# First expert weights in 32 tensors, and the expert numbers of the last tiles read once, two tiles ahead

## The reference

```
x = x + attention(layernorm(x))            # 4 heads, dk 128, dv 64, a scan over 512 tokens
h = layernorm(x)
probs = softmax(h @ router_w.T)            # 8 experts
vals, idx = top_k(probs, 2)
out = 0
for e in range(8):
    w = sum(where(idx == e, vals, 0), -1)
    out += w[:, None] * (gelu(h @ w1[e].T) @ w2[e].T)   # w1[e]: 1024 x 256, w2[e]: 256 x 1024
x = x + out
```

## Time and profile before

| | us |
|---|---|
| median of three executions | 939.12 |
| the profiled execution | 941.82 |
| its span, first to last instruction | 940.0 |
| PE busy | 860.5 (92%) |
| VectorE busy | 627.1 (67%) |
| ScalarE busy | 604.0 (64%) |
| GpSimd busy | 440.4 (47%) |
| mean granted TensorE clock | 0.972 |

### The profile page before, as it was taken

One profiled execution on the slowest core, in us unless ns is written; L12 is line 12 of the kernel. 1 busy time (PEld: TensorE's weight loads), 2 busy tenths in 40 slices (PEclk: granted clock), 3 DMA queues, 4 the chain that ended last, 5 costly groups with the idle time before them and its releaser, 6 DMA issues. The chain is left out here.

```text
span 940.0 us, 29903 instructions
## 1 busy us (share of the span) xinstructions
PE 860.5 (92%) x9998; PEld 677.0 (72%) x9999; DVE 627.1 (67%) x1832; ACT 604.0 (64%) x1645; POOL 440.4 (47%) x433
## 2 busy tenths in 40 slices
PE   3789999999999999999987899999999999998883
PEld 2468887788877888788866677777777777766661
DVE  4578898698988989888874845555554555543441
ACT  3478888788888888888776644555544555433430
POOL 2164555577677677677556532233322233312222
PEclk9899999899999999999987999999999999999997
DMA  6012322233233332332232342233322223312212
GB/s 207 2 58 80 87 64 76 74 98 96 89 103 89 96 104 82 102 103 76 70 108 91 127 69 47 46 49 57 50 47 45 45 45 59 52 29 47 35 18 29
DMA packets 50152, 66.96 MB, mean 71 GB/s; under 512 B 6448, under 2 KB 34352, under 8 KB 50032
## 3 DMA queue, kind: packets, MB, share of 16 engines
q1 hardware_dynamic: 36064, 46.20, 17.1%
q0 software_dynamic: 13424, 18.10, 11.2%
q10 hardware_dynamic: 544, 1.05, 0.3%
HBM read 41.84 MB, written 23.48 MB: 69 GB/s over the span
## 5 line engine op out<-in xcount | busy, mean ns | idle before, releaser
L764 ACT ACTIVATE inverse_levels<-ps 128x512 f16<-128x512 f32 (+1 forms) x324 | 169.7, 539 | 181.6 <-PE ps L1499 154.8
L746 POOL DMA_INDIRECT out<-inverse_levels,yidx x71 | 119.0, 1676 | 277.8 <-DVE inverse_levels L2180 194.8
L1126 PE MATMUL ps<-inverse_levels,w_hi 128*128 128x256 f16 (+1 forms) x1376 | 199.6, 255 | 1.5 <-issue 1.3
L1126 PE MATMUL ps<-inverse_levels,w_lo 128*128 128x256 f16 (+1 forms) x688 | 169.2, 254 | 0.0
L2153 DVE SCALAR_TENSOR_TENSOR KpAT<-kq_wvg,inverse_levels 128x512 f16<-128x512 f32 (+1 forms) x144 | 98.8, 688 | 95.2 <-ACT inverse_levels L764 95.1
L1126 PE MATMUL ps<-w_s,inverse_levels 128*128 x426 | 141.3, 381 | 14.9 <-ACT inverse_levels L764 9.0
L1126 PEld LDWEIGHTS ps<-inverse_levels,w_hi 128*128 x1376 | 119.7, 98 | 19.0 <-issue 2.4
L1126 PE MATMUL ps<-w_s,KpAT 128*128 x426 | 116.6, 274 | 0.0
L1026 ACT ACTIVATE kq_wvg<-ps 128x512 f32<-128x512 f32 (+1 forms) x144 | 85.0, 590 | 46.4 <-PE ps L1126 40.3
L2176 DVE TENSOR_SCALAR inverse_levels<-ps,gate 128x256 f32<-128x256 f32 x71 | 31.1, 480 | 102.8 <-PE ps L1126 102.8
L1734 DVE CAST_PREDICATED inverse_levels<-mask_s,ps 128x256 f16<-128x256 int8 x192 | 82.2, 428 | 18.0 <-PE ps L1126 12.7
(11 more groups left out here) (237 smaller groups left out, 1932.3 us busy)
## 6 DMA issues: line engine op xcount, KB each, us to landing
wst<-w SPq DMA_DIRECT2D x58, 256.0 KB
inverse_levels<-eye SPq DMA_DIRECT2D x35, 256.0 KB, 2.7
x_s<-x SPq DMA_DIRECT2D x32, 128.0 KB, 2.6
out<-x_s SPq DMA_DIRECT2D x32, 128.0 KB, 1.7
x_s<-routed_rows SPq DMA_DIRECT2D x7, 260.0 KB, 2.7
Lh<-routed_rows SPq DMA_DIRECT2D x7, 260.0 KB, 2.7
Vp<-routed_rows SPq DMA_DIRECT2D x7, 260.0 KB, 2.9
rowA<-routed_rows SPq DMA_DIRECT2D x7, 260.0 KB, 2.9
```

The costliest lines, as they stand in the source:

```text
L746: pool.indirect_dma_start(out=out, out_offset=bass.IndirectOffsetOnAxis(ap=yidx[:, q, a:a + 1], axis=0), in_=yrow[:, q % 2, a, :], in_offs ...
L764: return act.activation(dst, src, ACT.Copy, scale=scale)
L1126: return pe.matmul(dst, lhsT, rhs, start=start, stop=stop, **kw)
```

## The change

Three things change.

The two tensors w1_hi and w1_lo become 32, one for each part, k and m, of eight experts by 128 columns. The host lays out w1 in the new order, so that the pieces that are loaded are still 64 of 512 columns, and `split_hi` and `split_lo` write each to its place (`w1_place`).

In `up` the address of a weight is taken from the tensor of its part, k and m at e * 128.

For split tiles `parts_of` no longer reads the expert numbers. `load_experts(t + 2)` reads them in `down` of tile t, behind the fifth of the eight blocks m (m = 4), and keeps them for `up` and `down` of that tile.

```
-        w1_hi = sb("w1_hi", [P, KC * E * HID], fp16)
-        w1_lo = sb("w1_lo", [P, KC * E * HID], fp16)
+        w1_hi, w1_lo = [[[sb(f"w1_{part}_{k}_{m}", [P, E * P], fp16) for m in range(KH)] for k in range(KC)] for part in ("hi", "lo")]
...
+        def w1_place(at):
+            n = E * P // PIECE
+            return at // (KH * n), at // n % KH, slice(at % n * PIECE, (at % n + 1) * PIECE)
...
-                    cols = slice(at * PIECE, (at + 1) * PIECE)
-                    lo, hi, src = w1_lo[:, cols], w1_hi[:, cols], wst[:, :]
+                    k, m, cols = w1_place(at)
+                    lo, hi, src = w1_lo[k][m][:, cols], w1_hi[k][m][:, cols], wst[:, :]
...
+            loaded = {}
+            def load_experts(t):
+                if t < TILES and split(0, t):
+                    loaded[t] = [(expert_of(*divmod(t, 4), a), slice(a * P, (a + 1) * P)) for a in range(halves(*divmod(t, 4)))]
             def parts_of(i, q):
+                if split(i, q) and i * 4 + q in loaded:
+                    return loaded[i * 4 + q]
...
                         for k in range(KC):
-                            off = e * HID + (k * E * HID + m * P)
-                            wh, wl = w1_hi[:, bass.ds(off, P)], w1_lo[:, bass.ds(off, P)]
+                            wh, wl = w1_hi[k][m][:, bass.ds(e * P, P)], w1_lo[k][m][:, bass.ds(e * P, P)]
...
                         last = mm(p_yo[a][:, 0, :], hlo[:, q % 2, m, a * P:(a + 1) * P], w[:, 0:D], False, m == KH - 1)
+                    if m == KH // 2 and isinstance(i, int):
+                        load_experts(i * 4 + q + 2)
```

More of the change, by code:

```diff
@@ L920, in split_hi @@
                 if which == 0:
-                    dst, src = w1_hi[:, at * PIECE:(at + 1) * PIECE], wst[:, :]
+                    k, m, cols = w1_place(at)
+                    dst, src = w1_hi[k][m][:, cols], wst[:, :]
                 else:
@@ L2336 @@
     fconst, iconst = constants()
-    w1 = g["L0_ffn_w1"].transpose(2, 0, 1).reshape(KC, P, T // KC, PIECE).transpose(0, 2, 1, 3).reshape(T, P, PIECE)
+    w1 = g["L0_ffn_w1"].transpose(2, 0, 1).reshape(KC, P, E * P // PIECE, PIECE // P, KH, P).transpose(0, 4, 2, 1, 3, 5).reshape(T, P, PIECE)
     w2 = g["L0_ffn_w2"].transpose(2, 0, 1).reshape(KH, P, T // KH, PIECE).transpose(0, 2, 1, 3).reshape(T, P, PIECE)
```

## The result

| | before | after |
|---|---|---|
| median of 4 runs each | 939.31 us (938.82 to 940.28) | 925.31 us (923.38 to 929.25) |
| ratio, 95% interval | | 0.9864 (0.9835 to 0.9892) |
| profiled execution | 941.82 us, span 940.0 | 925.97 us, span 924.2 |
| mean granted clock | 0.972 | 0.977 |
| seven full split `up`s with the gap behind each | 57.74 us | 46.40 us |

The forecast was 928.6 in 924.0 to 932.0.

The account below looks back on a forecast made before the run. PE's sequencer, issuing address operations and expert-number reads, was taken to bound split tiles. Reads 7.7 plus 2.8 us in seven `up`s (addresses, fuller queue) gave 10.5 us, so 928.6 us, within 924.0 to 932.0.

Parts of the forecast that it names:

- The bound: Split tiles: PE's sequencer, 0.255 us a triple against PE's 0.168, paces `up` from half; reads make the 1.30 us gap behind.
- The rival that PE itself is slow on 128 columns: Split `up`: 73 ns a matmul is PE's own pace, so only the gaps go: 931.4 us; chance 0.03.
- Part 1: Ahead of `down` of tiles 28 to 33: six reads of 1.29 us, during which PE stands still, go: 7.7 us.
- the fuller queue: Start of split `up`: 16 pairs queued instead of 14 to 15, half a triple less to issue afterwards.
- the second rival: Split `up`: addresses save nothing; only 7.7 and 0.1 to 0.2 each from the queue are left: 930.4 us; chance 0.13.
- The 0.16 us that were to be left of the gap: Between split `up` and `down`: one semaphore and one register operation remain, 1.45 - 1.29 = 0.16 us.
- Part 2: Two reads moved behind the fifth block of `down` cost nothing, covered by the sequencer's lead of 1.6 us.
- the rival in which the reads stop PE: `down`s of tiles 26 to 33: a read waits for an empty queue, 9.7 us new standstill: 938.3 us; chance 0.04.
- Part 3: Split `up`: two ALU_OPs replace FUSED_REGOPS and ALU_OP, saving 14 ns a triple, 0.255 to 0.241 us.
- The PE-bound rival: Split `up`: the ALU_OP is as cheap as the w_lo step looks, `up` takes 5.4 us: 920.9 us; chance 0.09.
- Part 4: Layout: pieces, their size and evacuation shapes stay, cost 0; could cost only in the first stage, on ACT and POOL.
- The tail: From tile 33's rows POOL's five additions set the end; earlier savings count in full; the 6.2 us landing: 1.6 either way.

Follow-up runs that it names:

- fused pair: The change, with both weight addresses of a split-tile triple computed together by one FUSED_REGOPS instead of two ALU_OPs: 914.72 us, again 917.03 us.
- Reads only: The kernel before with only the change's moved expert-number reads, w1 still in two tensors: 925.3 us, ratio 0.9855.
- double reads: The change with every expert number of a split tile read twice in a row in the middle of `down`: 931.27 us, ratio 0.9914.
- late reads: The change with its reads moved from the middle of `down` to its last block: 926.73 us, ratio 0.9858.
- three operations: The change with one more ALU_OP per split-tile triple, the second matmul reaching the same weights through its own register: 950.45 us, ratio 1.0125.
- Old layout with the fused pair: The kernel before with the moved reads and both addresses of a triple computed together, w1 in two tensors: 914.01 us, ratio 0.9728.
- before again: The kernel before the change, nothing altered, profiled a second time: 947.92 us, ratio 1.001.
- addresses only: The change without its moved reads: w1 in 32 tensors, expert numbers read ahead of `up` and again ahead of `down`: 933.86 us, ratio 0.9957.
- old reads with the fused pair: The change with both addresses of a triple in one FUSED_REGOPS, but reads ahead of `up` and `down` as before: 921.04 us, ratio 0.9807.
- the change, again: The changed kernel, nothing altered, run and profiled a second time: 925.47 us, ratio to before 0.9844.

## Why the prediction was right, point by point

**The bound.** That PE's sequencer paces a split `up` from its middle, and the reads the gap behind, holds: one operation more per triple lengthened the triple by 110 ns, one fewer made PE the bound at the 5.4 us that the start of an `up` had shown. (My first sentence misread: PE's slices also fall to 8, 7 and 8 around the end of the first stage. Nothing in the sum rests on it.) The rival that PE itself is slow on 128 columns is out: 55.8 ns over 96 matmuls in the fused pair. The Trainium skill (TensorE: Matmul & The Clock Gate, Back-to-back issue gap) has some 81 ns there for loads and matmuls in turn; the trace, with 96 weight loads among these 96 matmuls, disagrees.

**Part 1, reads ahead of `down`: 7.7 forecast.** The gap is gone in every tile. Reads only gained 9.14 us in the windows: in each of the later six 8.32 - 6.83 = 1.49 us, 1.29 of it the reads and 0.20 left for the fuller queue. The first window, which keeps its read ahead of `down` (that of the pair tile 27), shows that term by itself: 7.81 - 7.62 = 0.19 us. So the second rival had priced it rightly (0.1 to 0.2 each), and the sum had not: of its 0.40 us per `up` 0.37 are the address, which leaves 0.03. This is the term that was mis-sized: some 1.4 us in seven windows where the sum had 0.2. The 0.16 us that were to be left of the gap did not show: 6.56 us against 6.55 busy.

**Part 2, cost nothing, lead 1.6 us.** Right, and the lead measured by double reads. In the changed kernel each `down` of a split tile takes 5.21 us as before, so the rival in which the reads stop PE is out. The stop at 16 pairs is seen in the split `up`s of all nine profiles in which they were counted: outstanding pairs rise to 16 and no further. At the start of an `up` the kernel before got to 13 to 16, the changed one to 16 each time. The Trainium skill (Advanced Engine Details and Errata, Engine Queue Depths) has 64 entries; the trace shows half of that in loads and matmuls together. The choice of place, which I had argued from the lead, made no difference (late reads).

**Part 3, addresses: 14 ns a triple, 0.37 of the 0.40 us per `up`.** Beside the reads the addresses brought (48.60 - 7.62 - 46.40 + 7.23) / 6 = 0.30 us a window, without them 0.34: 11 to 13 ns for each of 26.7 triples. The rule used, a fixed surplus of some 0.085 us for each operation whatever its kind, gives 0.117 for an ALU_OP; three operations measured 0.110. The rule holds for two, four or six instructions behind the operation, but not for none: in a read, TENSOR_LOAD (0.307 us), FUSED_REGOPS and SEQ_ASSERT follow one another with only 0.06 us over each record (849.844, 850.209, 850.418 in the kernel before). The PE-bound rival failed on this step: the ALU_OP was no cheaper than its record said. The second rival (addresses save nothing) is out.

**Part 4, layout: 0.** Old layout with the fused pair and new layout give the same windows, pair tiles the same 5.24. The first stage shows no cost either: it ended at 538.89 us with the old layout and the fused pair, at 537.62 and 539.96 with the new one.

**The tail: 1.6 either way.** Here is the term that was wrong in kind. I took the landing of 6.2 us for chance, as likely after as before, and put it at nothing in the sum. It was 6.24, 6.28 and 6.12 us in the three profiles with the reads ahead of `down` and two single operations for a triple (before, before again, addresses only), and 4.5 to 5.1 in all the others. So 1.2 to 1.7 us of the gain belong there. It isn't simply the period: three operations has tiles still farther apart (15.7 us) and lands in 4.62. The DMA packets tell more. In the kernel before, 139 of the addition's 144 packets have started 3.34 us after its issue, and the last five start only at 4.41. In between one packet of 16 KB of the instruction queue keeps one of the 16 DMA engines busy (6.2%) for 0.98 us. The queues that move anything from 918.30 to 919.28, and from 919.25 to 920.20:

```profile
q8 instruction: 1, 0.02, 6.2%
```

```profile
q0 software_dynamic: 5, 0.00, 5.3%
```

Before again and addresses only show the same: the last 5 and 9 packets start at 4.45 and 4.18 us, as a packet of the instruction queue ends (4.47 and 4.20). So does an earlier addition of old reads with the fused pair, which lands in 5.64 us. In the other profiles that packet fell earlier or later, or held nothing up (in the change, again, it ran from 3.07 to 4.11 us). That the late packets stood behind it on one DMA engine is my reading; no run moved the packet. But it fits a delay that comes back in the same kernel and goes away when the timing changes a little. Nothing in the change aimed at it, so this part of the gain is luck.

**The sum.** 11.3 in the windows (10.5 forecast) and 1.4 in the tail are 12.7 of the 14.0 between the medians; in the profiled pair another 3.1 lie ahead of the pair stage. The 1.3 that are left are inside the interval of the ratio (2.7 us either way), and I assign them to nothing. Split up, the windows' 11.3 are 7.7 for the reads (7.7 forecast), some 1.4 for the fuller queue (0.2) and 2.2 for the addresses (2.6). Of the other signs, the period of a split tile fell to 12.20 us (12.3 forecast), the first window to 7.23 (7.4), the reads from 28 to 13 (some 15), and PE's waits on ACT from 9.0 to none (0.5).

The mechanism was right, and most of the gain is its work. The median, 925.31 us, lies inside the stated range but below the forecast's own one of 926.5 to 930.5: of the 3.5 us by which 14.0 exceed 10.5, 0.8 were in the windows, 1.4 in the tail, which could have come with either sign, and the rest in nothing that a run shows. That the sum of such terms stayed inside the wide range is in part luck.

## What to carry to other kernels

Count the sequencer's operations for a group of matmuls (here each took its record plus some 80 ns, 0.11 to 0.14 us) against what PE needs for the group; where the first is larger, put address computations side by side so that they issue as one operation, before changing layouts. A read of a register from memory (0.65 us with its check) was free here wherever the queue held that much work, and cost its full time where the sequencer was already behind. And measure an effect of a few microseconds in the windows of its own stage: here they repeat to 0.1 us, while the medians carry several microseconds of other stages.

## What the hardware showed that I had not expected

- What a FUSED_REGOPS holds is nearly free: two additions record 37 ns, additions with multiplications 55 to 60, and the surplus of some 80 ns comes once. Where the queue had room, the fused operations of one `up` followed each other in 115 ns (854.676, 854.791 and 854.906 in the fused pair), and 133 ns with the old layout, both below PE's 168; two ALU_OPs took 225.
- A lead that was spent on reads from a full queue came back within 1.1 us, at no cost (late reads: 8 pairs outstanding at 860.47 us, 16 at 861.58, PE at the `up` at 862.34).
- One packet of the instruction queue, 16 KB in 0.98 us, goes with a landing that is 1.2 to 1.7 us longer, and a landing stands in the tail in full.
- The same kernel took 938.2, 939.2, 939.9 and 946.6 us on four chips, and its split stage 57.74 and 57.84 us in the two profiles.
